# Rotary layers on one core: the sine product in one instruction, key normalisation on GpSimd, queries copied by halves

## What is computed

```
q = l2norm(q) * qs;  k = l2norm(k) * ksc
q = q * cos * scale + rotate_half(q) * sin * scale
k = k * cos * inv   + rotate_half(k) * sin * inv
out = local_attention(q, k, v)          # softmax over 64 keys
x = attn_layer(shift_tokens(x), ...) + x
x = ffn_layer(shift_tokens(x), ...) + x
```

## Time and profile before

| | |
|---|---|
| time, median of 3 runs | 4228.52 us (4224.45 to 4230.75) |
| the profiled execution | 4228.07 us, its span 4226.3 us |
| mean granted clock of the matrix engine | 0.991 of full speed |
| PE busy | 3943.4 us (93%) |
| VectorE busy | 3877.6 us (92%) |
| ScalarE busy | 2604.9 us (62%) |
| GpSimd busy | 2692.1 us (64%) |

### The profile page before, as it was taken

One profiled execution on the slowest core, in us unless ns is written; L12 is line 12 of the kernel. 1 busy time (PEld: TensorE's weight loads), 2 busy tenths in 40 slices (PEclk: granted clock), 3 DMA queues, 4 the chain that ended last, 5 costly groups with the idle time before them and its releaser, 6 DMA issues. The chain is left out here.

```text
span 4226.3 us, 124870 instructions
## 1 busy us (share of the span) xinstructions
PE 3943.4 (93%) x48616; PEld 2737.1 (65%) x48616; DVE 3877.6 (92%) x4836; ACT 2604.9 (62%) x3780; POOL 2692.1 (64%) x4716
## 2 busy tenths in 40 slices
PE   7999999997999999999999999999999999999996
PEld 4666666665666666666666666666666666666664
DVE  5888888887899999999999999999999999999994
ACT  4666666653566666666666665666666666666663
POOL 5565556545667676676667666666676666666663
PEclk9999999999999999999999999999999999999999
DMA  5454554540000001000110001100011000010000
GB/s 136 93 100 94 98 98 93 103 98 20 24 17 15 20 29 29 17 15 17 31 29 16 16 16 30 29 18 15 16 30 29 20 15 16 20 38 20 15 16 14
DMA packets 342441, 165.08 MB, mean 39 GB/s; under 512 B 114241, under 2 KB 337473, under 8 KB 341185
## 3 DMA queue, kind: packets, MB, share of 16 engines
q1 hardware_dynamic: 342208, 161.99, 17.3%
HBM read 115.67 MB, written 33.69 MB: 35 GB/s over the span
## 5 line engine op out<-in xcount | busy, mean ns | idle before, releaser
L630 POOL TENSOR_TENSOR pn<-es,rden 128x1024 f32<-128x1024 f32 x192 | 366.3, 1908 | 695.3 <-DVE rden L959 695.3
L726 ACT ACTIVATE y<-ps 128x1024 f32<-128x1024 f32 x384 | 372.2, 1021 | 511.1 <-PE ps L1205 511.1
L634 POOL TENSOR_TENSOR t<-t 128x1024 f32<-128x1024 f32 x192 | 454.5, 2367 | 79.8 <-DVE t L911 79.8
L911 DVE TENSOR_TENSOR t<-ps,tabl 128x512 f32<-128x512 f32 x768 | 491.0, 681 | 0.0
L678 ACT ACTIVATE t<-ps,amx 128x512 f32<-128x512 f32 x512 | 347.5, 688 | 224.6 <-DVE amx L815 224.6
L909 DVE TENSOR_TENSOR t<-ps,tabl 128x1024 f32<-128x1024 f32 x384 | 467.2, 1217 | 8.0 <-ACT sq L749 4.3
L636 POOL TENSOR_TENSOR t<-t 128x1024 f32<-128x1024 f32 x192 | 452.8, 2358 | 4.4 <-DVE t L911 4.4
L1013 DVE TENSOR_TENSOR qn<-t,rn 128x2048 f32<-128x2048 f32 x192 | 438.1, 2282 | 5.6 <-POOL rn L399 5.6
L969 DVE TENSOR_REDUCE ss<-sq 128x32 f32<-128x2048 f32 x192 | 437.0, 2276 | 0.0
L1054 PEld LDWEIGHTS ps<-cst,qn 128*128 128x128 f32 x3072 | 350.2, 141 | 118.6 <-issue 61.7
L815 DVE TENSOR_REDUCE amx<-ps 128x2 f32<-128x1024 f32 x256 | 310.9, 1214 | 109.9 <-PE ps L1076 109.6
(11 more groups left out here) (134 smaller groups left out, 8224.5 us busy)
## 6 DMA issues: line engine op xcount, KB each, us to landing
wm<-values_dram SPq DMA_DIRECT2D x128, 256.0 KB, 5.1
y<-values_dram SPq DMA_DIRECT2D x128, 256.0 KB, 4.9
values_dram<-qT SPq DMA_DIRECT2D x64, 256.0 KB, 2.3
tokens_dram<-x SPq DMA_DIRECT2D x96, 128.0 KB
xs<-tokens_dram SPq DMA_DIRECT2D x192, 64.0 KB, 1.8
xw<-tokens_dram SPq DMA_DIRECT2D x192, 64.0 KB, 1.8
xsh<-x SPq DMA_DIRECT2D x48, 128.0 KB
xsh<-x SPq DMA_DIRECT2D x48, 127.0 KB
```

Source lines behind the costliest of these rows:

```text
L630: nc.gpsimd.tensor_tensor(heads(pn[:], H), heads(es[:], H), rden[:].unsqueeze(2).to_broadcast([P, H, KEYS]), ALU.mult).then_inc(l_p, 1)
L634: nc.gpsimd.tensor_tensor(t1[:, 0:INNER], t1[:, 0:INNER], t2[:, 0:INNER], ALU.add).then_inc(l_rotq, 1)
L726: return act.activation(y[:].rearrange("p h (w q) -> p w h q", w=NW)[:, 2 * half:2 * half + 2], src.rearrange("p (w h q) -> p w h q", w=2, ...
L911: sine = nc.vector.tensor_tensor(t23[:, :, lo:lo + DH // 2], q3[:, :, hi:hi + DH // 2], tabl[:, 1, u, i, lo:lo + DH // 2].unsqueeze(1).to_ ...
```

## The change

Three edits in the layers. First, `rotate` writes the sine product in one instruction of 1024 elements, whose input is read with the halves of each head swapped by a negative step. Second, VectorE multiplies only the queries by the reciprocal norms (1024 elements); the keys' half is done by GpSimd after its Newton steps, with a semaphore `l_kn` of its own, on which the matrix engine waits before it transposes the keys. Third, the matrix engine signals after 4 and after 8 transposes of the queries, and ScalarE copies them in two instructions of one bank each; the output product waits only for the first.

```diff
@@ gpsimd turn, after the Newton steps
+                if s.has(3):
+                    pool.wait_ge(l_rotk, t + 4)
+                    pool.wait_ge(l_rs, (t + 4) * RS_POOL)
+                    past(pool, l_tk, t + 3)
+                    nc.gpsimd.tensor_tensor(heads(qn[:, INNER:2 * INNER], H), heads(t1[:, INNER:2 * INNER], H),
+                                            rn[:, H:2 * H].unsqueeze(2).to_broadcast([P, H, DH]), ALU.mult).then_inc(l_kn, 1)
@@ scalar turn
-                    act.wait_ge(l_tq, t + 3)
                     past(act, l_s, t + 2)
-                    act.activation(qT[:].rearrange("p h c -> p (h c)"), pool0, ACT.Copy).then_inc(l_qT, 1)
+                    for half in range(2):
+                        act.wait_ge(l_tq, 2 * t + 5 + half)
+                        act.activation(qT[:, 4 * half:4 * half + 4].rearrange("p h c -> p (h c)"), bank(half),
+                                       ACT.Copy).then_inc(l_qT, 1)
@@ rotate
-                for lo, hi in ((0, DH // 2), (DH // 2, 0)):
-                    sine = nc.vector.tensor_tensor(
-                        t23[:, :, lo:lo + DH // 2], q3[:, :, hi:hi + DH // 2],
-                        tabl[:, 1, u, i, lo:lo + DH // 2].unsqueeze(1).to_broadcast([P, H, DH // 2]), ALU.mult)
-                sine.then_inc(done, 1)
+                swapped = src.rearrange("p (h s d) -> p h s d", h=H, s=2)[:, :, ::-1, :]
+                nc.vector.tensor_tensor(t23.rearrange("p h (s d) -> p h s d", s=2), swapped,
+                                        tabl[:, 1, u, i].rearrange("p (s d) -> p s d", s=2).unsqueeze(1)
+                                        .to_broadcast([P, H, 2, DH // 2]), ALU.mult).then_inc(done, 1)
@@ vector turn
                     dve.wait_ge(l_sqk, t + 4)
+                    past(dve, l_kn, t + 3)
                     rotate(1, u, pool1, l_rk)
...
-                    dve.wait_ge(l_rotk, t + 4)
-                    past(dve, l_tk, t + 3)
-                    nc.vector.tensor_tensor(heads(qn[:], 2 * H), heads(t1, 2 * H),
-                                            rn[:].unsqueeze(2).to_broadcast([P, 2 * H, DH]), ALU.mult).then_inc(l_qn, 1)
+                    past(dve, l_tq, 2 * t + 6)
+                    nc.vector.tensor_tensor(heads(qn[:, 0:INNER], H), heads(t1[:, 0:INNER], H),
+                                            rn[:, 0:H].unsqueeze(2).to_broadcast([P, H, DH]), ALU.mult).then_inc(l_qn, 1)
@@ tensor turn
-                    transposes(0, pool0, qn[:]).then_inc(l_tq, 1)
+                    for half in range(2):
+                        transposes(0, pool0, qn[:], half).then_inc(l_tq, 1)
+                    pe.wait_ge(l_kn, t + 3)
                     past(pe, l_y0sb, t + 1)
                     transposes(1, pool2, qn[:]).then_inc(l_tk, 1)
                 if s.has(0):
...
-                        pe.wait_ge(l_qT, t + 3)
+                        pe.wait_ge(l_qT, 2 * t + 5)
...
```

More of the change, by code:

```diff
@@ L289, in build @@
         l_qn = sem("l_qn")
+        l_kn = sem("l_kn")
         l_tq = sem("l_tq")
@@ L1050, in project, with transposes @@
                 return m
-            def transposes(i, pool, src):
-                for a in range(PAIRS):
+            def transposes(i, pool, src, half=None):
+                for a in range(PAIRS) if half is None else range(half * 4, half * 4 + 4):
                     t = nc.tensor.transpose(pool[:, a * P:(a + 1) * P], src[:, i * INNER + a * P:i * INNER + (a + 1) * P], ident)
@@ L1270, in turn @@
                     if s.has(2):
-                        pe.wait_ge(l_qT, t + 3)
+                        pe.wait_ge(l_qT, 2 * t + 6)
                     past(pe, l_xT, t + 4)
```

## The result

The changed kernel takes 4270.55 us, the median of 4 runs (4268.56 to 4276.15), against 4228.69 us before: a ratio of 1.0104, with a 95% interval of 1.0092 to 1.0116. The forecast was 4277, slower by 49 us; measured are 42. The profiled execution has a span of 4266.7 us, with a mean granted clock of 0.982 (0.991 before).

What follows compares the result with a forecast made beforehand. VectorE was taken as the bound, with the matrix engine in step and about 0.35 us of room a turn. +28.5 + 27.5 - 2 - 5 = +49 us on 4228.07 gave 4277 us; range 4210 to 4322.

Steps and rivals of the forecast that it cites:

- The bound and the exclusion: VectorE slightly ahead as bound; its instructions with two SBUF inputs and GpSimd's exclude each other whole, first started goes first.
- The order in c = 2 and 3: GpSimd's key product starts before VectorE's query product, which waits 1.65 us: +0.39 us in about 73 turns, +28.5 us.
- c = 0 and c = 1: Key product in c = 0 delays GpSimd's feed-forward Newton steps and c = 1: +27.5 us, and -2 us from c = 0 turns.
- The copy by banks: Matrix engine's 0.35 us wait before its output product goes, shortening only some 15 turns: -5 us.
- (A): In c = 2 and 3 GpSimd's product starts over 0.41 us after Newton and comes second: 4222 us, chance 0.13.
- The sine product: In the rotation, one instruction for two saves 0.12 us a turn, of which 0.06 reaches the turn's end.
- (B): No exclusion between the two normalisation products, or VectorE always first: faster, 4167 us, chance 0.09.
- (C): Slower swapped read, key product of 2.38 us, or feed-forward Newton steps held longer: from 4310 us upwards, chance 0.15.
- (D): In c = 1 the floor L971 slips between GpSimd's two sums: gain within 10 us, inside the forecast's 0.63 chance.

Runs made afterwards that it cites:

- the two repairs and no filling: Changed kernel with VectorE's query product first in c = 1 to 3 and VectorE multiplying the keys in c = 0: 4198.87 us, ratio 0.9944.

## Why the prediction was right, point by point

**The bound and the exclusion** held: VectorE's query product is 1.22 us wide where it is free and 2.66 us in c = 2 and 3, and it changes with the order of the two products, not with their sizes.

**The order in c = 2 and 3** was right, the size a third too large. Forecast was +0.45 us from the query product to the sums; measured are 2.59 to 2.60 us against 2.28 (medians), +0.32. Two terms were mis-sized. The gap between the last Newton step and the key product was taken from L649 as 0.16 us; it is 0.09 us (1880.83 to 1880.92), about the 0.08 between two Newton steps, so the second, satisfied wait cost nothing here. And the sums' record starts 0.08 us ahead of the blocked product's end. The time from release to end, 1.09, measured 1.08. With the sine's 0.06 a steady turn got longer by 0.25 us, not 0.39. There were about 80 such turns, 20 us in place of 28.5.

**c = 0 and c = 1** went step by step as forecast. The first feed-forward step runs, the second is blocked; L652 starts 10.09 us after the guess, L645 started 9.17 after it before (2427.35), +0.92 for +0.88; the floor waits 2.09 us for "about 2"; the whole step from c = 0 to c = 1 got longer by 0.78 us for +0.77. The waits also come out in the turns themselves: in batches without a fold and without a clock drop, c = 0 and 1 together take 34.94 us against 34.23 before, +0.71 where the forecast had +0.77 - 0.06. But half of these batches are of another kind, which the prediction did not have: the clock drop delays the exponentials and VectorE by about 0.85 us, so the floor waits only 1.06 us, and the two turns take 35.17. The +0.77 for the step between the query products is therefore reached partly by luck: it is the mean of +0.5 without a drop and +1.1 with one. The experiment that takes the product out of c = 0 gave 50 us, more than this term's 27.5 less 2, since it frees other gains as well.

**The copy by banks.** Some 15 turns were to gain 0.35 us each, 5 us in all. In c = 2 and 3, 14 turns in which the matrix engine is the bound got shorter, but by 0.56 to 0.87 us each, 9 us in all. Alone the copy gave 12 us. The prediction itself had said for rival (A) that the exponentials in steady turns come with the matrix engine, and did not count that here. That it would lengthen the engine's idle time in c = 0 and lower its clock was missed; this costs 19 us in the changed kernel.

**The sine product** had the right duration, and 5 us in place of the 11 that were in the sum.

**The sum, turn by turn.** Adding up all turns of both traces, from softmax sums to softmax sums, c = 2 and 3 grew by 11 us, where the forecast's terms make 28.5 - 5 = 23.5. c = 0 and 1 grew by 34 us, where they make 27.5 - 2 = 25.5; with the filling transposes it is 20 us, so some 14 of the 34 go with the clock. The exclusion and its two places are shown; that the total came so near (+42 for +49) is in part luck, since the conflict in c = 2 and 3 was sized too large and the clock, left out, made up for most of that.

**The rivals.** (A) would have needed a gap of 0.41 us where 0.09 stands. Its total, 4222, is near the 4217.5 of the run with VectorE first, but not by its own terms: a steady turn of c = 2 or 3 gained 0.17 us there, not 0.35. (B) is out by the products of 2.66 us. (C): GpSimd's product has its row's 1.90 us (median 1902 ns), and the sine product 1.22. Its sum had a slip: 0.48 us in 109 turns are 52 us, not 51. The prediction's estimate of 2.25 us comes from the 4497 ns that the Trainium skill's page "GPSIMD Engine Reference", section "Performance versus the Vector engine", gives for 2048 elements, measured on an addition; it is 18% too high for this product with a broadcast operand. (D) occurred in 1 of 44 turns; in the steady ones without a drop the key sum had been running for 0.31 us when the floor came, for the forecast's 0.35. The page "SBUF — State Buffer" of the Trainium skill, section "SBUF: two separate sides", says that of two such instructions the one that starts first takes the shared port pair for its whole length. The trace agrees with its 2.66 us behind the key product, and the run with VectorE first, where the same product takes 1.22.

## What to carry to other kernels

Before work is moved from VectorE to GpSimd in a kernel like this one, list VectorE's instructions with two SBUF inputs and ask which of them will meet the moved one; if they meet, make the engine with idle time go second by a wait, and keep the moved work out of turns in which a chain on GpSimd is due. Count the gain only up to the next late input: here an instruction shorter by 1.15 us had 0.04 us to give until the exponentials came earlier. And where a faster engine gets more idle time in one place, look at the matrix engine's granted clock there.

## What the runs showed of the hardware that was not expected

The matrix engine's idle time in c = 0, once in four turns, grew by 0.7 us. At 1.7 us none of 45 was followed by a half-speed stretch; at 2.3 to 2.4 us it was 20 of 44 in the changed kernel, 14 of 45 with the copy alone and 18 of 45 with the two repairs and no filling. Twelve transposes, 0.12 us apart, in this gap removed the drops, worth 19 us in one kernel and 30 in the other (4198.9 to 4168.5). And VectorE's multiplication reads a PSUM operand whose outer step is negative, over runs of 32 elements, as fast as the plain order: 1213 ns for 1024 elements, against 1215.
